# Two-layer conditional network on one core: a scalar-engine cast and a tanh moved, and the first layer's transposes reordered

## The reference, cut to what matters

```python
# first layer, one batch at a time; fside F is 128 x 16
z = x @ F @ F.T / (128 * 16)
x1 = x + gelu(x @ W.T + fc_bias + z + cond)
# second layer
logits = mean_parts(x1) @ gate_w ...          # one row of 4 per batch
w_be = top2_of_softmax(logits)                # weights of the 4 experts
out = x1 + shared_mlp(x1) + sum_e w_be[:, e] * mask[e] * mlp_e(x1)
```

## Time and profile before

| | us |
|---|---|
| median of 3 runs | 241.34 (241.19 to 241.63) |
| the profiled execution, whole | 241.15 |
| its span, first to last instruction | 238.9 |
| PE busy | 231.5 (97%) |
| DVE busy | 200.5 (84%) |
| ACT busy | 142.7 (60%) |
| POOL busy | 19.4 (8%) |

### The profile page before, as it was taken

How to read it: one execution, slowest core, us unless ns; L and a number is a source line. 1 busy time by engine, 2 the same in 40 slices (tenths; PEclk the granted TensorE clock), 3 DMA queues, 4 the chain that set the end, 5 groups by cost and what they waited for, 6 DMA issues and landing times.

```text
span 238.9 us, 3425 instructions
## 1 busy us (share of the span) xinstructions
PE 231.5 (97%) x1194; PEld 197.4 (83%) x1194; DVE 200.5 (84%) x456; ACT 142.7 (60%) x279; POOL 19.4 (8%) x46
## 2 busy tenths in 40 slices
PE   8999899999999999999999999999999999999995
PEld 7886587788788887888798887888888889899894
DVE  0389999999896867976899998996999989778883
ACT  3598999816965097743977179443654075553531
POOL 8000000014000020002000030002000030020000
PEclk9999999999999999999999999999999999999999
DMA  6993000000010000100000000100010000100011
GB/s 181 293 287 95 3 0 0 3 0 0 3 44 0 0 0 4 44 0 1 3 33 11 0 3 1 44 0 3 0 44 0 3 0 1 44 3 1 0 44 44
DMA packets 11256, 7.40 MB, mean 31 GB/s; under 512 B 3776, under 2 KB 10600, under 8 KB 11240
## 3 DMA queue, kind: packets, MB, share of 16 engines
q1 hardware_dynamic: 10760, 7.07, 10.0%
q0 software_dynamic: 192, 0.03, 0.2%
q10 hardware_dynamic: 288, 0.10, 0.2%
HBM read 5.09 MB, written 2.10 MB: 30 GB/s over the span
## 4 chain that ended last, share of the span: by engine, by line
PE 75%; ACT 12%; DVE 9%; issue 2%; POOL 0%; DVEq 0%; ACTq 0%; POOLq 0%
PE ps L521 23%; PE ps L523 22%; PE ps L522 22%; ACT h L428 5%; DVE hs_lo L815 2%; PE ps L527 2%; PE ps L539 2%; ACT L428 2%; ACT L409 2%; PE ps L570 1%; ACT W_raw L414 1%; PE ps L664 1%; DVE segsum L790 1%; PE ps L578 1%; ACT hs_hi L443 1%
## 5 line engine op out<-in xcount | busy, mean ns | idle before, releaser
L428 ACT ACTIVATE h<-ps,b_col 128x512 f32<-128x512 f32 (+1 forms) x160 | 90.6, 640 | 58.8 <-PE ps L523 55.5
L833 DVE SCALAR_TENSOR_TENSOR hs_lo<-h,w_be,hs_hi 128x344 fp32r<-128x344 f32 (+1 forms) x124 | 73.5, 654 | 0.0
L521 PE MATMUL ps<-x_hi,W_hi 128*128 128x512 f32 (+2 forms) x168 | 66.0, 393 | 2.7 <-ACT hs_hi L431 1.4
L523 PE MATMUL ps<-x_lo,W_hi 128*128 128x512 f32 (+2 forms) x168 | 60.8, 362 | 0.0
L522 PE MATMUL ps<-x_hi,W_lo 128*128 128x512 f32 (+2 forms) x168 | 60.7, 361 | 0.0
L521 PE MATMUL ps<-hs_hi,W_hi 128*128 128x512 f32 (+1 forms) x156 | 57.2, 367 | 0.4 <-DVE hs_lo L833 0.4
L523 PE MATMUL ps<-hs_lo,W_hi 128*128 128x512 f32 (+1 forms) x156 | 56.9, 365 | 0.0
L522 PE MATMUL ps<-hs_hi,W_lo 128*128 128x512 f32 (+1 forms) x156 | 56.6, 363 | 0.0
L825 DVE TENSOR_SCALAR hs_hi<-h,w_be 128x344 fp32r<-128x344 f32 (+1 forms) x120 | 44.9, 438 | 8.4 <-PE ps L523 4.2
L521 PEld LDWEIGHTS ps<-x_hi,W_hi 128*128 128x128 f32 x168 | 31.7, 189 | 12.1 <-ACT h L428 2.9
L522 PEld LDWEIGHTS ps<-x_hi,W_lo 128*128 128x128 f32 x168 | 31.8, 189 | 4.3 <-issue 1.0
(11 more groups left out here) (121 smaller groups left out, 178.3 us busy)
## 6 DMA issues: line engine op xcount, KB each, us to landing
W_raw<-in_L_cond_ew SPq DMA_DIRECT2D x8, 256.0 KB, 5.7
out<-x_tok SPq DMA_DIRECT2D x7, 256.0 KB, 2.1
x_tok<-in_x SPq DMA_DIRECT2D x3, 512.0 KB, 6.2
x_tok<-in_x SPq DMA_DIRECT2D x2, 256.0 KB, 3.4
W_raw<-in_L_cond_sw SPq DMA_DIRECT2D x2, 256.0 KB, 4.6
out<-x_tok SPq DMA_DIRECT2D x2, 128.0 KB, 1.7
F_pad<-in_fside_Bx1x1024x SPq DMA_DIRECT2D x2, 64.0 KB, 5.6
W_raw<-in_L_cond_W ACTq DMA_DIRECT2D x1, 64.0 KB, 2.9
```

The costliest lines, as they stand in the source:

```text
L428: ins = nc.scalar.activation(span(h[:, k % 3, c, :], s), up_bank(k, c), ACT.Gelu_apprx_tanh, bias=b1_col[:, s, c:c + 1])
L521: nc.tensor.matmul(dst, w_hi, m_hi, start=start, stop=False)
L523: return nc.tensor.matmul(dst, w_hi, m_lo, start=False, stop=stop)
L833: nc.vector.scalar_tensor_tensor(lo[:, :, c], h[:, k % 3, :, c], w_be[:, t * NB + b, s - 1:s], f32(hi[:, :, c]), ALU.mult, ALU.subtract).t ...
```

## The change

On ACT, `x1_high(1)` moves from behind the loop over the front's tiles to behind `weight_high` of tile 1, that is ahead of `gelu0(2)`; and `gelu(1)` goes ahead of `gate_tanh(0)`. On DVE, `split(0)` goes ahead of `read_logits(0)` and `gate_maximum(0)`. On PE, the four matmuls on ones are taken out of `matrices`; `xT(1)` goes ahead of `matrices(0)`, `xT(2)` ahead of `matrices(1)`, and in the loop `layer0(t)` comes first, then `xT(t+3)`, `matrices(t+2)`, `transpose_F(t+3)`. No DMA and no buffer is changed.

```diff
@@ ACT @@
                     x1_high(0)
                 if t < 2:
                     weight_high(WEIGHTS[t + 2])
-            x1_high(1)
+                if t == 1:
+                    x1_high(1)
             act.wait_ge(b1_ok, 1)
             gelu(0)
+            gelu(1)
             gate_tanh(0)
-            gelu(1)
@@ PE @@
             def matrices(t):
-                if t < 2:
-
-                    keep_busy(2)
                 if t >= NA:
...
             transpose_F(0)
             pe.wait_ge(W_in, 16)
             nc.tensor.transpose(psWT, W_raw[:, :], ident[:, :]).then_inc(WT_ps, 1)
+            xT(1)
             matrices(0)
-            xT(1)
             transpose_F(1)
             pe.wait_ge(cond_in, 16)
             pe.wait_ge(WT_ok, 1)
             nc.tensor.transpose(psCondT, cond_raw[:, :], ident[0:B, 0:B]).then_inc(condT_ps, 1)
+            xT(2)
+            matrices(1)
+            transpose_F(2)
             for t in range(NA):
-                if t + 1 < NA:
-                    matrices(t + 1)
+                layer0(t)
+                if t + 3 < NA:
+                    xT(t + 3)
                 if t + 2 < NA:
-                    xT(t + 2)
-                    transpose_F(t + 2)
-                layer0(t)
+                    matrices(t + 2)
+                if t + 3 < NA:
+                    transpose_F(t + 3)
@@ DVE @@
             modulation()
+            split(0)
             read_logits(0)
             gate_maximum(0)
-            split(0)
             gate_ranks(0)
             split(1)
```

## The result

The changed kernel took a median of 245.10 us (244.49 to 246.11, 6 runs) against 241.26 (240.50 to 241.63, 6 runs) for the kernel before: a ratio of 1.0166 (95% interval 1.0144 to 1.0188). Ratios, here and in the table of experiments, leave out runs more than 1.5% above the fastest of the same kernel (of those in which the clock fell, both of e8, one of four in e9 and all three of e3, which so has no ratio), while medians and ranges count every run. The forecast was 241.8, with a range to 242.6. It was wrong; one of the rivals, the fall of the clock, at 0.08, is what came. The profiled execution took 246.11, with a span of 243.9 us.

The account below looks back on a forecast made before the run. PE's work sets the pace behind the front, which DVE ends, with `residual(0)` as hinge. Ones -0, `xT(1)` -0.5, `xT(2)` waiting +0.96, ACT 0 gave +0.46 on the 241.34 median: 241.80, range 240.7 to 242.6.

Parts of the forecast that it names:

- the fall of the clock: Rival, chance 0.08: PE's clock falls in the hole ahead of `xT(2)`, +2.4 us, giving 243.7.
- What bounds the front: DVE ends the front; the end moves with `residual(0)`, behind PE's chain to `layer0(0)`, +0.46 us there.
- ACT's and DVE's edits at 0: Moving `x1_high(1)`, `gelu(1)` and `split(0)` was put at 0, since DVE ends the front.
- `xT(1)` forward, a gain of 0.5: On PE, `xT(1)` fits into the wait ahead of `matrices(0)`, so `matrices(1)` could start 0.5 us earlier.
- `xT(2)` waits for its load: PE would stand still from 8.5 to 10.03 until the x load lands, holding up `matrices(1)` and `layer0(0)`: +0.96 us.
- The +0.46: Net delay in us at `residual(0)`: -0 for the ones, -0.5 for `xT(1)`, +0.96 for `xT(2)` waiting.
- the last rival: The wait swallows a front's late clock start, so the loss is taken up and medians come closer: 241.4, chance 0.15.
- The ones at 0: Both pairs of ones on PE fill waits for ACT; removal gains at most 0.05 and 0.08 us, put at 0.
- The section on the clock: A clock fall in the hole ahead of `xT(2)` would make the end 2.4 us later, at most 3.5.
- the stretch behind the last matmul: Window from 237.90 at the kernel's end: clock 0.59 after some 1.5 us in which PE had nothing.
- The factor of 1.6: Slowdown at the lower clock, from first transposes taking 1.06 us against 0.66 later, applied to `xT(2)` through `layer0(0)`.
- the rule cited in the prediction: Idle stretches of TensorE waiting for a DMA send the clock back to half, and the matmuls behind pay.

Follow-up runs that it names:

- e8: Kernel before without the first pair of ones, ahead of `matrices(0)`, the second kept: 241.28 us, ratio 0.9995, 2 of 10 runs fell.
- e9: Changed kernel with both pairs of ones left at the head of `matrices(0)` and `matrices(1)`: 242.17 us, ratio 1.0041, 4 of 12 runs fell.
- e3: Kernel before without the two pairs of ones and nothing else: 246.78 us, 3 of 4 runs fell, no ratio.
- e1: Changed kernel with four matmuls on ones ahead of `xT(2)`, in the wait for its data: 241.40 us, ratio 1.0011, no falls in 10 runs.
- e4: Kernel before with the edits of ACT and DVE alone, PE's list as before: 241.00 us, ratio 0.9992.
- e5: Changed kernel with SP issuing `load_x(2)` and `load_F(2)` ahead of the first two weights, no ones: 240.00 us, ratio 0.9971, 3 of 10 runs fell.
- e11: e6 run a second time, the same kernel: 240.78 us, ratio 0.9987, no falls in 12 runs.
- e10: e6 with ACT's and DVE's lists as in the kernel before: 240.80 us, ratio 0.9977, no falls in 12 runs.
- e2: Changed kernel with `xT(2)` behind `matrices(1)` again, no ones: 242.17 us, ratio 1.0023, 6 of 10 runs fell.
- e7: Changed kernel with `xT(2)` behind `matrices(1)` and two matmuls on ones ahead of `matrices(1)`, loads as before: 240.70 us, ratio 0.9994, 3 of 12 runs fell.
- e6: e5 with one matmul on ones ahead of `xT(2)` and one behind it: 240.04 us, ratio 0.9964, no falls in 8 runs.

## Why the prediction was wrong

**What bounds the front: right.** The end was said to move with `residual(0)`, and `layer0(0)` ahead of it. In the profiled executions in which the clock stayed up, the span less the start of `layer0(0)` is 238.9 - 11.68 = 227.2 before, 239.0 - 11.66 = 227.3 in e1, 239.5 - 12.13 = 227.4 in e4, 237.1 - 9.92 = 227.2 in e5, 238.7 - 11.32 = 227.4 in e11, and 240.2 - 12.87 = 227.3 in e9: within 0.2 us, while `layer0(0)` moves by 3.0 us.

**ACT's and DVE's edits at 0: right,** by e4 and by e10 against e11. The figures of ACT held: the table load directly behind gelu0(3), a hole of 0.53 before the tanh for the half us said.

**`xT(1)` forward, a gain of 0.5: right.** In e2 and e7 it is the only gain left, and their runs with a whole clock have medians of 240.5 and 240.6 against 241.2, 0.6 to 0.7 us less.

**`xT(2)` waits for its load: right in kind, somewhat large in size.** The load landed at 9.86 in the changed kernel (issue 3.83 + 6.03) and the first transposes at 9.90. The +0.46 assumed 10.03 for the landing; with the loads in this order, landings of 9.5 to 10.3 were seen. The hole was 0.91 us and not 1.5, as PE came to it at 8.99 and not at 8.53: `xT(1)` at 6.13 still took 1.06 us, as at the lower clock. In e1 PE was there at 8.53, as predicted. Against the medians of before, e1 has +0.14 to +0.18, with runs from 241.15 to 241.62 where the kernel before beside it had 240.37 to 241.71. That is the 241.4 of the last rival, by which the wait swallows a late start of the clock. It fits, but no run tests it apart from the landing.

**The ones at 0: the step that failed.** The prediction weighed them as work and as time, found both pairs lying in waits for the copy of F, and put their removal at 0 (a gain of at most 0.13 us). What they gave was the clock: without them, and nothing else changed, three of four runs fell (e3). With four of them in the wait, none of ten fell in the changed kernel (e1), where without them six of six did. The section on the clock had the right mechanism, down to the purpose of the ones, but looked at the one hole ahead of `xT(2)` and set its chance to 0.08 on the strength of the stretch behind the last matmul, where the clock held for 1.5 us. That row was a poor guide for the front. There, holes of 0.5 to 0.9 us stood ahead of a fall in three kernels (changed, e2, e3). Why the end held longer than the front is not shown by any run.

**Its price was mis-sized too.** The rival counted the low clock until the end of `layer0(0)`, for +2.4 us and 243.7. Up to there the sum came out, in part by luck: `residual(0)` is 2.42 us late, with `xT(2)` at 9.90 instead of 10.12, but 15.15 - 9.90 = 5.25 us from there to the end of `layer0(0)` instead of 3.1 + 1.9 = 5.0. The factor of 1.6 compares durations; between starts, `matrices(1)` and `layer0(0)` took 1.8 and 1.7 times as long. But the low clock lasted until about 21 us. From `residual(0)` to `down(2)` the profiled execution took 46.30 - 16.36 = 29.94 us, against 41.57 - 13.94 = 27.63 before: 2.3 of the 4.7 us were lost behind the point at which the prediction stopped counting, 0.99 and 1.16 of them in DVE's two later waits.

**The hole and the rule.** In the changed kernel 0.91 us of idle time came before a clock of 0.50. By the rule cited in the prediction from the Trainium skill (TensorE: Matmul & The Clock Gate, "HAM oscillation"), idle time in which TensorE waits for a DMA sends the clock back and the matmuls behind it pay. The trace agrees in kind, and goes further: the waits of that section's example are several times as long as this one. In e3 the waits are mostly for ACT's copy, and the clock fell as well.

**What helps.** Of the change, the forward move of `xT(1)` is sound, and that of `xT(2)` does no harm if its load goes ahead of the first weights and ones stand beside it (e6, e10, e11: no fall in 32 runs). That it gains anything over `xT(1)` alone is not shown: the runs of e7 that kept the clock have a median of 240.6, between those of e6 and e11. The ones have to stay, in the waits. The version of e6 and e11 is 0.1 to 0.4% faster than the kernel before, by its two ratios, and some 1.9% faster than the changed one (240.4 between its two medians, against 245.1).

## What to carry to other kernels

Matmuls that compute nothing are not free to remove because they lie in a wait: ask what the engine does for the clock in that stretch, and keep it fed until the dense part begins. Before a piece of work is moved forward in an in-order list, look up when its data lands; a load that nobody waits for today can be the next wait, and everything behind it in the list waits too. And price a fall of the clock over the whole stretch of light work that follows, not over the pieces next to the hole: here it lasted from 3 to 17 us.

## What the runs showed of the hardware

- Idle stretches of PE of 0.50 us (e2), of 0.61, 0.54 and 0.31 us (e3) and of 0.91 us (changed) came before a fall from 2.4 to 1.2 GHz; one of 1.2 us in the profiled execution of e9 did not. The same program fell in some runs and not in others, and what decides between them is open.
- A busy PE did not bring the clock back soon: with no idle time at all it stayed at 0.50 from 11 to 14 us (e2), to beyond 20 (changed) and to 27 (e3). In e3 the first matmuls of 512 columns, at 25.82 to 27.25, still took 0.63 to 0.77 us, against 0.39 to 0.40 from 28.02 on.
- The first matmuls of every kernel run at the duration of the lower clock, and the moment at which this ends differs from run to run (the four transposes at 4.12 us take 0.60 in e3, those at 6.13 take 1.06 in the changed kernel). Between e6 and e11 `layer0(0)` differs by 0.87 us with it, and it is the likely, though not separately tested, source of the spread of the kernel before, 240.3 to 241.8.
